# Second attention, first two blocks: the second batch's turns two steps down, the last two swaps ahead of the row scaling, and one wait moved to its first use

## What is computed

```python
q = (hidden_states @ Wq).reshape(b, t, NH, D).transpose(0, 2, 1, 3)
k = (hidden_states @ Wk).reshape(b, t, NKV, D).transpose(0, 2, 1, 3)
v = (hidden_states @ Wv).reshape(b, t, NKV, D).transpose(0, 2, 1, 3)
...
q = q * cos + _rotate_half(q) * sin
k = k * cos + _rotate_half(k) * sin
...
attn = jnp.einsum('bhtd,bhsd->bhts', q, k) * scale
attn = jnp.where(causal, -jnp.inf, attn)
attn = jax.nn.softmax(attn, axis=-1)
out = jnp.einsum('bhts,bhsd->bhtd', attn, v)
out = out.transpose(0, 2, 1, 3).reshape(b, t, NH * D)
return out @ Wo
...
x = x + _L1_attn_ref(_layernorm(x, axis=-1), ...)
```

## Time and profile before

| | us |
|---|---|
| median of 3 runs (969.53 to 971.62) | 969.66 |
| the profiled execution, its own time | 971.26 |
| its span, first to last instruction | 969.1 |
| PE busy in the span | 898.3 (93%) |
| DVE / ACT / POOL busy | 730.2 / 620.9 / 361.0 |

### The profile page before, as it was taken

The page is one execution under the profiler, slowest core; times in us unless marked ns, Lnnn a source line. Parts: engine busy times, 40 slices in busy tenths (PEclk is TensorE's granted clock), DMA queues, the critical chain, the costliest instruction groups (busy, mean ns, idle before and its releaser), DMA issues.

```text
span 969.1 us, 17521 instructions
## 1 busy us (share of the span) xinstructions
PE 898.3 (93%) x6208; PEld 583.1 (60%) x6208; DVE 730.2 (75%) x1499; ACT 620.9 (64%) x1251; POOL 361.0 (37%) x401
## 2 busy tenths in 40 slices
PE   3689999999999999998799999999999999898998
PEld 1313222322222232455689889888998899787897
DVE  7799999999999998668655554555455547797877
ACT  3267888888888888544755656555555554365665
POOL 5700000000000010121675869296929683247422
PEclk9779999999999999899799999999999999999999
DMA  2410111111000000000000000000000012000000
GB/s 68 139 50 25 33 54 40 40 37 32 23 20 24 18 1 18 1 1 18 1 1 1 1 18 1 2 15 4 1 1 2 1 29 60 1 1 12 12 12 12
DMA packets 23375, 20.10 MB, mean 21 GB/s; under 512 B 5177, under 2 KB 17441, under 8 KB 23289
## 3 DMA queue, kind: packets, MB, share of 16 engines
q1 hardware_dynamic: 23288, 18.99, 6.8%
HBM read 14.26 MB, written 4.59 MB: 19 GB/s over the span
## 4 chain that ended last, share of the span: by engine, by line
PE 63%; DVE 23%; POOL 7%; issue 4%; ACT 2%; DMA 1%; SPq 0%; DVEq 0%; POOLq 0%; ACTq 0%
DVE halves L831 15%; PE a_sum L2228 9%; PE summed L1045 7%; PE m_down L2484 6%; PE score_bank L1032 5%; PE a_turn L2213 4%; PE max_bank L992 4%; PE a_scores L1734 3%; PE max_bank L1005 3%; PE a_scores L1735 3%; PE a_scores L1736 3%; POOL a_rotated L1828 2%; POOL a_crossed L1826 2%; PE m_hid L2302 1%; PE m_hid L2303 1%
## 5 line engine op out<-in xcount | busy, mean ns | idle before, releaser
L956 ACT ACTIVATE probs<-score_bank 128x512 f32<-128x512 f32 x512 | 267.8, 601 | 75.4 <-PE score_bank L1032 75.2
L831 DVE TENSOR_REDUCE halves<-max_bank 128x2 f32<-128x1024 f32 x256 | 298.6, 1219 | 11.0 <-PE max_bank L992 8.9
L2228 PE MATMUL a_sum<-a_v,a_turned 128*128 128x128 f32 x1152 | 165.2, 280 | 2.4 <-ACT a_turned L2088 1.5
L1761 ACT ACTIVATE a_probs<-a_scores,a_lowest 128x896 f32<-128x896 f32 (+7 forms) x128 | 94.9, 742 | 109.7 <-DVE a_lowest L1756 108.8
L2228 PEld LDWEIGHTS a_sum<-a_v,a_turned 128*128 128x128 f32 x1152 | 145.6, 193 | 3.5 <-ACT a_turned L2088 2.1
L992 PE MATMUL max_bank<-k_stack,q_stack 48*128 48x512 bf16 x512 | 117.1, 397 | 25.0 <-DVE halves L831 24.8
L1045 PE MATMUL summed<-probs,v_tile 128*32 128x512 f32 x1024 | 138.5, 613 | 0.0
L1032 PE MATMUL score_bank<-q_stack,k_stack 50*128 50x512 bf16 x512 | 132.5, 386 | 3.8 <-ACT probs L956 2.3
L1756 DVE TENSOR_REDUCE a_lowest<-a_scores 128x1 f32<-128x896 f32 (+7 forms) x128 | 96.2, 755 | 30.9 <-PE a_scores L1738 29.9
L754 POOL COPY v_tile<-values 128x128 f32<-128x128 f32 x16 | 4.7, 294 | 303.7 <-PE summed L1045 303.2
L992 PEld LDWEIGHTS max_bank<-k_stack,q_stack 48*128 48x128 bf16 x512 | 25.2, 93 | 124.0 <-DVE halves L831 111.4
(11 more groups left out here) (343 smaller groups left out, 1628.8 us busy)
## 6 DMA issues: line engine op xcount, KB each, us to landing
rope<-in_rope SPq DMA_DIRECT2D x8, 256.0 KB, 3.1
rope<-in_L_ffn_mlp_w SPq DMA_DIRECT2D x8, 256.0 KB, 5.0
q_parts<-l_q_parts SPq DMA_DIRECT2D x2, 768.0 KB, 4.9
k_parts<-l_k_parts SPq DMA_DIRECT2D x2, 768.0 KB, 6.3
q_stack<-q_parts SPq DMA_DIRECT2D x30, 48.0 KB
k_stack<-k_parts SPq DMA_DIRECT2D x30, 48.0 KB
x<-in_L_attn_x SPq DMA_DIRECT2D x2, 512.0 KB, 4.1
q_stack<-shift SPq DMA_DIRECT2D x64, 2.0 KB
```

Source lines behind the costliest of these rows:

```text
L831: dve.reduce_max(halves[:, u % 2, half, :].rearrange("p (x t) -> p x t", x=2)[:, :, qt], max_bank[place % RING][:, :, :], AX_X).then_inc(f ...
L956: act.activation(probs[:, step % PROBS, x, :], score_bank[e % SCORES][:, :], ACT.Exp, scale=SCALE0).then_inc(prob_ready, 1)
L1761: act.activation(probs[:, k % 2, c, 0:row_width(n)], row_of(n), ACT.Exp, bias=lowest[:, n % 8:n % 8 + 1], accum_out=weight[:, k % 4, c:c + ...
L2228: last_use = pe.matmul(sum_bank[:, c * P:(c + 1) * P], turned[:, m % SLOTS, i * P:(i + 1) * P], v[:, b, first + i, q, :], start=(first + i ...
```

## The change

Four edits, all in head 0. (1) `READY`: the two *ready turn* and two *ready lower* events of block 0 move from steps 1 to 4 to steps 3 to 6. (2) Batch 1's first projection, at (0, 5), falls away there, and the one at (0, 7) is now the first; one is added at (1, 2), so that block 1 makes five in place of four, and from (1, 3) on the same unit stands at the same step. (3) In the prologue DVE does `straighten_next(4)` ahead of the aggregates and `straighten_next(5)` ahead of the inverse root; ACT does `swap_next(4)` ahead of rows 2 and 3 and `swap_next(5)` ahead of the row scaling. (4) The PE's wait for the second swap moves from turn 2 to use 0. No instruction with work in it is added or removed. POOL's and SP's queues hold the same instructions in the same order.

```diff
-READY = {(0, 1): ("turn", NCH // B), (0, 2): ("lower", NCH // B), (0, 3): ("turn", NCH // B + 1), (0, 4): ("lower", NCH // B + 1)}
+READY = {(0, 3): ("turn", NCH // B), (0, 4): ("lower", NCH // B), (0, 5): ("turn", NCH // B + 1), (0, 6): ("lower", NCH // B + 1)}
...
-            if units and j % 2 and not (first and k == 0 and j <= 4):
+            if units and (j % 2 or first and (k, j) == (1, 2)) and not (first and k == 0 and j <= 6):
                 placed = units.pop(0)
                 yield "project", placed
...
             take_lowest(1)
+            straighten_next(4)
             a1.aggregate(dve, chain, TB + 4, 2 * TB)
             take_lowest(2)
-            straighten_next(4)
             take_lowest(3)
+            straighten_next(5)
             a1.find_inverse(dve, chain, 1)
             a1.find_offset(dve, 1).then_inc(offset_found, 1)
-            straighten_next(5)
...
             take_value(3)
+            swap_next(4)
             exponentiate_first(2)
             exponentiate_first(3)
-            swap_next(4)
+            swap_next(5)
             act.wait_ge(offset_found, 1)
             scale_rows(FIRST)
-            swap_next(5)
...
-                        if g == 0 and m == USE_LAG:
-                            pe.wait_ge(swapped_ready, from_one(NROT))
...
+                        if g == 0 and m == 0:
+                            pe.wait_ge(swapped_ready, from_one(NROT))
                         if j == 0:
                             pe.wait_ge(out_taken, from_one(g * NB + k))
```

## The result

The changed kernel takes **980.33 us** (median of 6 runs, 978.34 to 983.05), the kernel before, beside it, 970.91 (6 runs, 969.53 to 972.38). The ratio is 1.0098, with a 95% interval from 1.0079 to 1.0117: slower by 9.4 us. That is above the predicted range of 970.0 to 976.0. The profiled execution took 980.21 us; its span is 978.1, against 969.1.

What follows compares the result with a forecast made beforehand. POOL's gapless chain, 20.2 us from its start to the first value unit, was taken as the bound. Its 3.2 us later start on the profiled 971.26 gave 974.5, carried over to the median as 972.9; range 970.0 to 976.0.

Steps and rivals of the forecast that it cites:

- Part 1: Prologue: root and straighten only change places, copy of turn 0 stays at 473.71, so turn 2 starts 1.74 us earlier.
- the five rivals: Outcomes for the whole kernel: late POOL chain 0.42, another clock fall 0.19, full clock 0.23, faster 0.07, no effect 0.09.
- rival (c): PE's restart at turn 2 (474.45) finds the full clock: +0.9 us, 970.6 us; chance 0.23.
- The reason given for a fall: PE's wait after turn 1: longer than the 2.0 us after which the clock fell before, so a fall is likelier.
- Part 3: Batch 1's first projection, now at (0, 7), starts POOL's chain 3.2 us later, and the first value unit with it.
- The signs named for it: From batch 1's projections on: POOL gapless, DVE stands at L1715 more than once, PE some 2 us ahead of first L1701.
- rival (b): POOL's chain late and clock falls again ahead of the value unit: +1.4 to +2.8 us on top; chance 0.19.
- The 3.2: Whole kernel: us added by POOL's later start, with the clock falling at turn 2; gives 972.9 us.
- (a): POOL's chain late, clock falling at the restart as before: 972.9 us; chance 0.42.
- how a fall should be priced: Slow stretch of 5.6 us at half clock: the skill's rule estimates 2.8 us, the prediction's steps 2.3; left undecided.

Runs made afterwards that it cites:

- e3: Changed kernel plus one wait that holds POOL's units 4 and 5 until the inverse root is done; 972.22 us, ratio 1.0024.
- e10: Kernel before with only the swaps and straightening of units 4 and 5 moved ahead, and POOL held until the root is done; 970.55 us.
- e8: Kernel before plus six unused products of two rope tables on POOL between its units 3 and 4; 977.08 us.
- e2: Kernel before with the changed turns and lower halves, projections and PE wait, but swaps and straightening left in place; 973.84 us.
- e4: Kernel before with only the projections changed: batch 1's first at (0, 7), one more at (1, 2); 975.06 us.
- e9: Kernel before plus twelve unused zero fills on POOL between its units 3 and 4; 972.27 us, a single run.
- e7: e6 with the first projections at (0, 6), (1, 0), (1, 2), (1, 3), (1, 5), (1, 7); 974.3 us.
- e6: Changed kernel with POOL held, turn copies and row 4's maximum and exponential ahead, turns only one step down, projections as in the kernel before; 970.14 us.
- e1: Kernel before with only the swaps and straightening of units 4 and 5 moved ahead, POOL left free; 978.24 us.
- e5: Kernel before with DVE's turn 0 copy ahead of the root, chunk 2's turn and lower half one step down, PE's swap wait at use 0; 975.71 us.

## Why the prediction was wrong, step by step

- **Part 1 failed at its first step.** "These two only change places", it said of the root and unit 5's `straighten`, and kept the copy of turn 0 at 473.71. It came at 478.54. The row durations of the root were taken as fixed, though the change let POOL's units 4 and 5 start beside it. The chain cost 5.2 us more (7.75 against 2.58), and turn 2 came 10.24 us behind row 3's maximum in place of 4.98. e3 and e10 give the chain's loss back with one wait on POOL; e8 produces it in the kernel before. The text ahead of the prediction says of the engines that they "meet only at semaphores". By these rows DVE and POOL also meet where no semaphore stands between them. I looked for what stood ahead of each instruction in its own queue, and for waits between queues, not for what runs *beside* it. None of the five rivals had it.
- **The rest of part 1 was right** where POOL keeps away: turn 2 at 5.07 us behind row 3's maximum in e2 and e3, forecast 4.98.
- **The clock in that place** stayed up in the profiles of e2 and e3, through 2.84 and 2.60 us of waiting, as in rival (c), whose "+0.9" at the value unit measured +0.97 and +0.75. The reason given for a fall, that the new wait is longer than the 2.0 us after which the clock fell before, is no rule: in e10 PE stood 3.67 us (470.17 to 473.84), the clock was 1.00 through the wait and until 475.0, and 0.50 from there. In the changed kernel the clock did fall in that place, as in the forecast, but behind a wait of 7.8 us.
- **Part 3 was right in mechanism**, and e4 shows it by itself. Its pieces also have the right size in the changed kernel. From turn 2 to the first projection 14.1 us were forecast and 13.63 measured, from there to POOL's start 2.91 and 2.99, from there to the value unit 20.2 and 20.19; in all 12 profiles the last is 20.18 to 20.22. POOL's start was 8.0 us later by the ruler where 3.2 were forecast, and this difference of 4.8 is the late turn 2 (5.26) less some 0.4 in the pieces behind it. The signs named for it are there too: three projections wait for a swap, 2.0 us in all, DVE stands behind POOL at L1715 three times, PE stands 1.88 us ahead of the value unit.
- **A second fall of the clock** is in the trace, at 835, but it isn't rival (b) come true. That rival had it ahead of the value unit, from the new idle time there. This one follows a wait that every kernel here has, and it is in e8 and e9 too, whose order on PE is that of the kernel before. That the change brought it is not shown.
- **The sum** of the spans is then 3.2 forecast, 4.8 from the late turn 2, 1.4 behind the value unit and -0.35 ahead of row 3: 9.0 us. The 3.2 is no cost that stands by itself, though. It rests on the clock falling at the restart. With POOL held (e3) the clock stayed up and the value unit was 0.75 us late, so of the 8.0 us up to it the one wait gives back 7.2: 5.2 from the chain and 2.06 with the clock.

**What stays open.** e2, e3 and e7 are 0.75 to 0.97 us longer up to the value unit, but 2.3 to 3.3 us longer by the ratios. Their profiles don't stand for all their runs: those of e2 and e7 took 971.01 and 971.75 us, and the medians are 973.84 and 974.3. The mean granted clock, which is on record for every run, divides them. In e2 the two runs with 0.982 took 970.45 and 971.01 us, the eight with 0.975 to 0.978 took 972.48 to 974.72. In e3 the five with 0.982 took 970.06 to 971.86, the five with 0.974 to 0.978 took 972.57 to 976.9. In e7 the one with 0.982 took 970.12, the nine with 0.973 to 0.977 took 971.75 to 976.38. So these kernels lose little in the runs with the high mean, and most of their loss is in the others. The mean alone doesn't explain it: the 19 runs of the kernel before that stand beside e2 took 968.84 to 971.57 us at 0.976 to 0.981. At 0.977 they took up to 971.56, e2 from 973.03 on. Some 3 us at the same mean clock is what the forecast gives with a fall at turn 2. Of the lower groups only the quickest runs of e3 (972.57) and e7 (971.75) were profiled: in e3 the clock was up at turn 2 and fell at 827.6, in e7 it was low from 474.9 to 478.3 and again from 826.4. Where it was low in the longer runs isn't known, so which of rivals (a) and (c) holds without the contention stays open.

Of the 12 profiles, the four without a fall behind the value unit (before, e4, e6, e10) have 460.3 to 461.2 us from there to the end, the other eight 461.9 to 462.7, 1.6 more between the means. These are different kernels, one execution each, so that is an estimate of what such a fall costs. A late first projection isn't its condition: e1, e5, e8 and e9 have such a fall without one of the moved projections.

The prediction left open how a fall should be priced. In the changed kernel 4.5 us had a mean clock of 0.62, and the end is 1.37 us longer than in the kernel before. By the rule of the Trainium skill, "TensorE: Matmul & The Clock Gate", section "Terms" (length times one minus the passed share), that is an estimate of 1.7 us. The trace is near to it; since the ends of the four kernels without a fall differ by 0.9 us among themselves, it can't say more.

## What to carry to other kernels

Before you let a transfer, a swap or any other releaser go earlier, ask which engine it sets to work and what runs *beside* that work, not only what waits for it. VectorE and GpSimd are the pair to look at. The case to fear is a chain of many tiny dependent steps: here, beside products, every second step was held to the end of a GpSimd instruction, 1.1 us and more for 0.17. If the GpSimd work has time to spare, one wait that holds it until the chain is through is the cheap cure (e3: 7 us).

A row of the kernel before could have warned: the small step L310 took 0.53 us and ended at 467.47, as POOL's L1818 ended (467.45). In the changed kernel the same step began in a gap of POOL's, at 467.18, and took 0.17.

```profile
466.84 0.61 POOL L1818 CAST m_room<-a_rotated 128x512 fp32r<-128x512 f32 x1
466.94 0.53 DVE L310 TENSOR_SCALAR a_token_of_root<-a_token_both 128x4 f32<-128x4 f32 x1
```

## What the runs showed of the hardware

- A DVE step on 128x8 elements takes 0.17 us alone and up to 1.26 us (e5) beside POOL's products of 128x512, ending when the POOL instruction ends. In the rows from 460 to 530 us of the changed kernel, e1 and e8 single products on POOL kept their 1.26 to 1.30 us, while two, two and one of its casts took 0.64 in place of 0.61. The side that was held for long was DVE each time.
- Beside POOL's fills of 128x512 (0.58 us each), TENSOR_SCALAR steps took 0.52 and 0.55 us, TENSOR_TENSOR and SCALAR_TENSOR_TENSOR steps 0.17.
- The same PE wait of 2.5 us (it ends at 824.6 to 834.6) was followed by the lower clock level within 1.3 us, or had it from its last 0.4 us on, in six executions (the changed kernel, e3, e5, e7, e8, e9). In the other six (before, e1, e2, e4, e6, e10) the clock stayed up; in e1 it fell 12 us later, with PE at work. What decides it isn't told by these rows.
- The clock stayed up through a PE wait of 3.67 us and fell 1.2 us after it (e10), and stayed up through and after waits of 2.84 and 2.60 us (e2, e3).
